# Second layer's expert loop: TensorE takes the pairs two at a time, and four buffers hold the activations

## The reference, cut to what matters

```
logits = x @ router_w                                  # 32 experts
probs = softmax(logits); topk_w, topk_idx = top_k(probs, 4)
g = einsum('th,ehi->tei', x, w_gate)                   # H = 256, I = 192
u = einsum('th,ehi->tei', x, w_up)
act = silu(g) * u
eo = einsum('tei,eih->teh', act, w_down)
routed = einsum('te,teh->th', combine, eo)
```

## Time and profile before

| | |
|---|---|
| median of 3 runs | 1363.02 us (1362.11 to 1373.45) |
| the profiled execution | 1364.06 us, its span 1362.3 us |
| PE busy over the span | 1260.1 us, 92% |
| DVE, ACT, POOL busy | 756.1, 675.0, 696.7 us |
| the expert loop, from its first up to its last result | 1094.9 to 1327.2 us |

### The profile page before, as it was taken

How to read it: one execution, slowest core, us unless ns; L and a number is a source line. 1 busy time by engine, 2 the same in 40 slices (tenths; PEclk the granted TensorE clock), 3 DMA queues, 4 the chain that set the end, 5 groups by cost and what they waited for, 6 DMA issues and landing times. The chain is left out here.

```text
span 1362.3 us, 25868 instructions
## 1 busy us (share of the span) xinstructions
PE 1260.1 (92%) x9066; PEld 953.3 (70%) x9066; DVE 756.1 (56%) x1606; ACT 675.0 (50%) x1511; POOL 696.7 (51%) x701
## 2 busy tenths in 40 slices
PE   4999838999999999999999679999799999999996
PEld 3777627888888888888888657777556645555444
DVE  6788764444444444444444346666485355555554
ACT  3777834545545445454454336656331155555552
POOL 6555213666666666666664433221038547776760
PEclk9999978999999999999999879999799999999998
DMA  6344422444444444444463355300100057777768
GB/s 232 56 63 64 93 100 95 109 108 109 108 108 108 108 108 105 106 105 104 105 164 49 67 195 191 113 18 2 64 1 1 24 171 224 224 224 220 223 182 308
DMA packets 145878, 161.97 MB, mean 119 GB/s; under 512 B 79333, under 2 KB 106603, under 8 KB 144496
## 3 DMA queue, kind: packets, MB, share of 16 engines
q1 hardware_dynamic: 111504, 106.50, 26.0%
q0 software_dynamic: 32256, 52.46, 18.6%
q10 hardware_dynamic: 2016, 1.71, 0.4%
HBM read 122.86 MB, written 39.85 MB: 119 GB/s over the span
## 5 line engine op out<-in xcount | busy, mean ns | idle before, releaser
L1282 POOL DMA_INDIRECT x_dram<-e_y,rows x128 | 218.2, 1705 | 191.8 <-ACT e_y L1390 167.1
L1317 PE MATMUL bank<-e_xg_hi,e_w_hi 128*128 128x512 f32 x512 | 159.1, 392 | 3.5 <-issue 2.0
L1425 DVE TENSOR_TENSOR e_hid<-e_sg,bank 128x512 f32<-128x512 f32 x128 | 88.0, 687 | 129.9 <-PE bank L1317 94.8
L1378 ACT CAST e_hidden_hi<-e_hid 128x512 fp32r<-128x512 f32 x128 | 79.5, 621 | 160.5 <-DVE e_hid L1425 160.5
L1221 POOL DMA_INDIRECT spare<-xn_dram,rows x128 | 125.1, 977 | 66.1 <-issue 38.4
L1317 PE MATMUL bank<-e_xg_hi,e_w_lo 128*128 128x512 f32 x512 | 158.2, 390 | 0.0
L1317 PE MATMUL bank<-e_xg_lo,e_w_hi 128*128 128x512 f32 x512 | 158.2, 390 | 0.0
L1428 DVE TENSOR_TENSOR e_hidden_lo<-e_hid,e_hidden_hi 128x512 fp32r<-128x512 f32 x128 | 88.6, 692 | 87.9 <-ACT e_hidden_hi L1378 87.9
L1953 PE MATMUL bank<-w,e_xT 128*64 128x384 f32 x320 | 116.5, 485 | 1.7 <-DVE e_wt L2055 1.7
L1953 PE MATMUL bank<-e_wt,e_xT 128*64 128x384 f32 x320 | 116.6, 486 | 0.0
L1390 ACT ACTIVATE e_y<-bank,shares 128x256 f32<-128x256 f32 x128 | 60.8, 475 | 106.5 <-PE bank L1330 106.1
(11 more groups left out here) (332 smaller groups left out, 2775.1 us busy)
## 6 DMA issues: line engine op xcount, KB each, us to landing
w<-in_L_ffn_w SPq DMA_DIRECT2D x48, 512.0 KB, 5.1
wgu<-in_L_gate_up SPq DMA_DIRECT2D x8, 1536.0 KB, 7.5
e_wd<-in_L_down SPq DMA_DIRECT2D x52, 192.0 KB
e_picked<-ys_dram SPq DMA_DIRECT2D x6, 1024.0 KB, 9.7
b_wq<-in_L_down SPq DMA_DIRECT2D x27, 192.0 KB
b_wk<-in_L_down SPq DMA_DIRECT2D x27, 192.0 KB
b_wv<-in_L_down SPq DMA_DIRECT2D x27, 192.0 KB
b_wo<-in_L_down SPq DMA_DIRECT2D x27, 192.0 KB
```

The source lines that it names most:

```text
L1282: nc.gpsimd.indirect_dma_start(out=x_dram[:, :], out_offset=bass.IndirectOffsetOnAxis(ap=rows[:, e, q:q + 1], axis=0), in_=y[q][:, :], in_ ...
L1317: last = nc.tensor.matmul(bank[f % 2][:, :], w[:, k * F0 + f * 128:k * F0 + (f + 1) * 128], x[:, k, h * SLOTS:(h + 1) * SLOTS], start=(w, ...
L1378: nc.scalar.copy(hidden[0][:, f, :], hid[f % 2][:, :]).then_inc(hi_sb, 1)
L1425: nc.vector.tensor_tensor(hid[f % 2][:, :], sg[f % 2][:, :], U_BANK[f % 2][:, :], ALU.mult).then_inc(hid_sb, 1)
```

## The change

TensorE's loop takes two pairs in a turn: both ups, the four turnings of `hid`, the four turnings of the token rows, both downs. ACT's and DVE's loops are rewritten to serve it in that order. `hid` has four buffers in place of two, and `up(t)` has a new wait, for `gated(t - 2)`, whose bank it overwrites. `turn_over` now runs two pairs further ahead of `up`: in the turn of `down(t)` stand `turn_over(t + 4)` and `turn_over(t + 5)`, where `turn_over(t + 3)` stood.

```diff
-        hid = [sb(f"hid{v}", [PT, F1]) for v in range(2)]
+        hid = [sb(f"hid{v}", [PT, F1]) for v in range(4)]
 ...
                 pe.wait_ge(xt_sb, t + 1)
+                if t >= 2:
+                    pe.wait_ge(hid_sb, t - 1)
 ...
-            turn_over(0)
-            turn_over(1)
-            up(0)
-            turn_over(2)
-            up(1)
-            turn_hidden(0)
-            for t in range(PAIRS):
+            for t in (0, 1):
+                turn_over(t)
+            for t in (0, 1):
+                up(t)
+            for t in (2, 3):
+                turn_over(t)
+            for t in range(0, PAIRS, 2):
                 if t + 2 < PAIRS:
                     up(t + 2)
-                if t + 1 < PAIRS:
-                    turn_hidden(t + 1)
-                if t + 3 < PAIRS:
-                    turn_over(t + 3)
+                    up(t + 3)
+                turn_hidden(t)
+                turn_hidden(t + 1)
+                if t + 4 < PAIRS:
+                    turn_over(t + 4)
+                    turn_over(t + 5)
                 down(t)
+                down(t + 1)
 ... (ACT)
-            take_hidden(0)
-            for t in range(PAIRS):
+            for t in range(0, PAIRS, 2):
                 if t + 2 < PAIRS:
                     gate(t + 2)
-                if t + 1 < PAIRS:
-                    take_hidden(t + 1)
-                if t + NBUF + 1 < PAIRS:
-                    take_weights(t + NBUF + 1)
+                    gate(t + 3)
+                take_hidden(t)
+                take_hidden(t + 1)
+                if t + 4 < PAIRS:
+                    take_weights(t + 4)
+                    take_weights(t + 5)
 ... (DVE)
-            for t in range(PAIRS):
-                if t + 3 < PAIRS:
-                    take_tokens(t + 3)
+            take_tokens(3)
+            for t in range(0, PAIRS, 2):
                 if t + 2 < PAIRS:
                     gated(t + 2)
+                    gated(t + 3)
+                if t + 4 < PAIRS:
+                    take_tokens(t + 4)
+                    take_tokens(t + 5)
+                    take_weights(t + 4)
                 take_result(t)
-                if t + NBUF + 1 < PAIRS:
-                    take_weights(t + NBUF + 1)
+                if t + 4 < PAIRS:
+                    take_weights(t + 5)
+                take_result(t + 1)
```

More of the change, by code:

```diff
@@ L1959, in turn_hidden @@
                 for m in range(2):
-                    last = nc.tensor.transpose(HT[t % 2][0:FH, m * PT:(m + 1) * PT], hid[t % 2][:, m * FH:(m + 1) * FH],
+                    last = nc.tensor.transpose(HT[t % 2][0:FH, m * PT:(m + 1) * PT], hid[t % 4][:, m * FH:(m + 1) * FH],
                                                r.ident[:, :])
@@ L2063, in gated @@
                 dve.wait_ge(sg_sb, t + 1)
-                nc.vector.tensor_tensor(hid[t % 2][:, :], sg[t % 2][:, :], GU[t % 2][:, F1:2 * F1], ALU.mult
+                nc.vector.tensor_tensor(hid[t % 4][:, :], sg[t % 2][:, :], GU[t % 2][:, F1:2 * F1], ALU.mult
                                         ).then_inc(hid_sb, 1)
```

## The result

The changed kernel takes 1477.52 us (median of 4, 1472.68 to 1480.46) against 1363.01 us: ratio 1.0816, interval 1.0771 to 1.086. It is slower by 8%; the forecast was 1462, with a range of 1425 to 1500. Its profiled execution took 1472.68 us with a span of 1471.0, so it is the fastest of the four, 4.8 us under their median. It is 108.6 us longer than the profiled execution of before, and the loop alone, from the first up to the end of the last down, is 107.7 us longer (1095.50 to 1435.0, against 1094.92 to 1326.73). All of the loss is in the loop.

A forecast was written before the change was run, and what follows sets the result against it. PE bounds the kernel at 2.88 us a pair; the change closes a loop through the gather, 8.41 us a turn against 5.76. 37 such turns add 98 us to 1364.1, less 1.5, plus 1 for the clock: 1462, range 1425 to 1500.

The forecast's parts named there:

- turning to the result's copy (1 to 3): From PE's turning of the odd pair's rows to the end of DVE's result copy, weights copied between: 2.30 us.
- copy to scatter: From the end of DVE's result copy to the start of POOL's scatter of that result: 0.80 us.
- scatter to gather: On POOL, from the scatter's start to the next gather's start: 1.08 us plus 0.30 us.
- landing: From the gather's start until its rows are there: 3.9 us, with ends of 3.2 and 4.3.
- Step 2: DVE copies the weights of t + 4 before the result of t: 0.90 us to that copy's start, 0.56 for it.
- Step 5: The odd pair's gather lands after 3.9 us, and PE resumes 0.03 us later.
- the collision with the down transfers: Down transfers of both pairs, issued right after the downs, fall on the gather; the median landing was still taken.
- a few falls: Falls of PE's granted clock in the loop, added to the forecast time as 1 us.
- a rival of 31 us (1493): PE's clock falls in each stall, so turning and down take twice as long: turn 9.25 us, time 1493; chance 0.14.
- the other turns and the tail: Three turns without a gathered odd pair gain 0.2 us each, and before's late gather and end wait vanish: -1.5 us.
- Faster: Rival: rows reach PE's turning in time and the grouping pays 8 us, giving 1356; chance 0.02.
- The rival of the down weights: Loads of down weights arrive late at down and set the turn: 20 us, 1384; chance 0.02.

The follow-up runs named there:

- busy_stall: Five unused matmuls put between the two turnings of token rows, against the changed kernel; 1471.56 us, ratio 1.0759 to the kernel before.
- gathers_first: POOL's order made two gathers, then two scatters, against the changed kernel; 1378.74 us, ratio 1.0077 to the kernel before.
- eight_buffers: Eight buffers for gathered rows in place of six, POOL's order untouched, against the changed kernel; 1365.53 us, ratio 1.0002 to the kernel before.

## Why the prediction was right

**The mechanism and the count.** The rows of the odd pair come behind a scatter of the turn before; 37 turns, none more. Two kernels that open the loop at POOL, one by order and one by buffers, and leave PE, DVE and ACT as changed, bring the median turn to 5.49 and 5.48 us and the time back to within 1%. That is shown.

**The sum of a turn: 8.41 forecast, 8.66 measured.** By its steps:

| step | forecast | measured, mean |
|---|---|---|
| turning to the result's copy (1 to 3), full clock | 2.30 | 2.13 |
| copy to scatter | 0.80 | 0.81 |
| scatter to gather | 1.38 | 1.32 |
| landing | 3.9 | 4.21 |
| resume | 0.03 | 0.04 |
| clock, in steps 1 to 3 | 0.03 | 0.14 |

The first measured value is that of busy_stall, where the clock is held up; the last is what the changed kernel takes more there (2.27); the others are of the changed kernel over 36 turns. They add up to 8.65. Step 2 was too long: of the two gaps in front of the weights' copy that the trace before offered, 0.48 and 0.31, the short one holds in this order. Step 5 was 0.31 too short, 11 us of the whole: the median of all landings is not that of those that PE will wait for. Half of this was in the trace before: it has landings for 62 of the 74 gathers, not for all, and those of the odd pairs took 4.05 on average. The forecast named the collision with the down transfers and then took the median all the same; the 4.3 of the later gathers, its upper end, was nearer. The errors of steps 2 and 5 partly cancel, which is luck, and part of why 8.41 comes near 8.66.

**The clock was given too little.** The forecast gave it 1 us, as "a few falls", and a rival of 31 us (1493) with a chance of 0.14 in which each turn lost it in full, 0.84 us. It took 5 to 10 us. The earlier trace rows put the fall at 2.2 us of rest, measured behind the loop. In the changed kernel it came after stalls of 1.8 to 2.5 us (the two read above) and while PE was working again. It came in half of the turns, and there often on work behind the critical copy, where it costs nothing. The Trainium skill, "TensorE: Matmul & The Clock Gate", section on HAM oscillation, tells of a kernel in which every wait for a transfer restarted the matmuls cold; here the clock did fall inside the turns (0.88), but in half of them only, and it cost at most a tenth of the loss, and the waiting itself the rest. 37 x (8.66 - 8.41) = 9.3 us is most of the distance from 1462 to the profiled 1472.7; of the 1.5 us expected back from the other turns and the tail nothing is seen. The median lies 4.8 above.

**Signs named ahead.** DMA share 0.53, measured 0.51. From a result to the odd gather 2.2 us, measured 2.12. 37 waits, found; but 74 us of them on PE and not 107, and PE busy for 0.77 and not 0.65 of the time. Both are the same thing: at half clock PE fills with longer matmuls a part of the time that it would have waited. A wait's total falls when the waiter slows down, and this was not thought of.

**What was put at nothing.** The new wait in `up`, the fourth buffer of `hid` and `take_hidden` closer behind its turning: with the loop open a clean turn has no gap at any of them: PE's own groups (2.58 + 0.57 + 0.44 + 1.90 in the turn of gathers_first above) make up the 5.49. POOL at 5.3 us in a turn did not bind at 5.47. The grouping gained 0.29 us in a turn and not 0.21: the up's 2.58 are two times the 1.29 of the earlier trace rows, so what it saves lies in the turnings and the downs.

**The rivals.** "Faster" needed the rows in time; eight_buffers had them in time and still was not faster, since the down weights then come late in some turns. (gathers_first had them in time in most turns.) The rival of the down weights (1384, each turn) was half right: it is the next bound, in some turns and not in all.

## What to carry to other kernels

Before a consumer is moved forward in its own order, follow its input back to the queue that issues it, and ask what that queue waits for just before: if it is a result of the same loop, add the whole round trip and compare it with the turn. The full cure lay on the issuing queue here (its order, or two more buffers); moving the turning back on the engine that stalls gave only 63 of the 114.5 us. And the cure gave back what was lost, no more: no kernel here was faster than the one before in a way that held when it ran again. Price a transfer by those that will be waited for, with the traffic that is issued beside them; here the landings that PE waited for took 0.5 us more than the median of all.

## What the hardware showed that was not expected

The granted clock fell behind rests of 1.8 and 2.5 us although PE had been fully busy for over 5 us between them, and the fall came 0.7 and 1.8 us after work had resumed. Five small matmuls in the middle of the stall kept it at 1.00 over 300 us. The gather of 128 KB landed in 3.04 us with little other traffic and in 4.20 next to transfers of 192 KB, while the gather issued 2.6 us behind it landed in 3.21 on average. The same kernel took 1364 to 1365 us on two chips, and 1424 and then 1405 on a third.
